# First gathers on edge numbers loaded for them alone, and a memset that follows only the first 190 early gathers, in a graph layer kernel

## The reference

```python
h = relu(layernorm(x))                                        # 100000 x 64
msgs_f = mlp_f([h[src], h[dst], edge_attr]); agg = segment_sum(msgs_f, dst)
msgs_r = mlp_r([h[dst], h[src], edge_attr]); agg += segment_sum(msgs_r, src)
return x + h + mlp_n([agg, h])                                # 100000 x 64
```

## Time and profile before

| what | value |
|---|---|
| runs | 1595.52, 1595.94, 1598.82 us; median 1595.94 |
| the profiled execution's own time | 1595.95 us |
| its span | 1594.2 us |
| POOL busy | 1102.0 us, 69% of the span |
| PE busy | 1280.9 us, 80% |
| DVE, ACT busy | 970.8 us, 942.6 us |
| DMA | 281.00 MB, 176 GB/s over the span |

### The profile page before, as it was taken

One profiled execution on the slowest core, in us unless ns is written; L12 is line 12 of the kernel. 1 busy time (PEld: TensorE's weight loads), 2 busy tenths in 40 slices (PEclk: granted clock), 3 DMA queues, 4 the chain that ended last, 5 costly groups with the idle time before them and its releaser, 6 DMA issues.

```text
span 1594.2 us, 29478 instructions
## 1 busy us (share of the span) xinstructions
PE 1280.9 (80%) x7070; PEld 969.6 (61%) x7070; DVE 970.8 (61%) x3294; ACT 942.6 (59%) x2256; POOL 1102.0 (69%) x1003
## 2 busy tenths in 40 slices
PE   5998998557888787878777788778678873999998
PEld 4777776335666565666555566556566652777776
DVE  7999999526666666666666666666666650222222
ACT  4888888434555455555455555555555442777776
POOL 7888888888888888888888888888888863000000
PEclk9999999767777888787888877877977786999999
DMA  6899998535555555555555555555555545999998
GB/s 217 292 315 315 314 315 279 161 49 111 111 112 111 111 99 102 104 104 103 105 105 105 105 104 99 106 102 99 101 102 105 104 78 156 382 370 369 364 367 297
DMA packets 238410, 281.00 MB, mean 176 GB/s; under 512 B 53170, under 2 KB 155200, under 8 KB 238348
## 3 DMA queue, kind: packets, MB, share of 16 engines
q1 hardware_dynamic: 168408, 241.57, 45.3%
q0 software_dynamic: 68992, 38.59, 21.5%
q10 hardware_dynamic: 948, 0.30, 0.1%
HBM read 162.62 MB, written 117.72 MB: 176 GB/s over the span
## 4 chain that ended last, share of the span: by engine, by line
POOL 36%; issue 21%; PE 18%; DMA 2%; DVE 1%; POOLq 1%; ACT 0%; ACTq 0%; DVEq 0%; SPq 0%
POOL table L532 30%; PE bank L871 6%; PE bank L882 6%; POOL got_odd L514 6%; PE bank L892 3%; DMA table<-to_send,scatter_at 2%; PE bank L820 1%; PE bank L846 1%; PE bank L818 1%; DVE same L979 0%; PE bank L833 0%; DMA same<-table 0%; ACT nh L639 0%; ACT to_send L625 0%; POOLq L530 0%
## 5 line engine op out<-in xcount | busy, mean ns | idle before, releaser
L532 POOL DMA_INDIRECT table<-to_send,scatter_at x392 | 623.5, 1591 | 134.7 <-issue 117.8
L846 PEld LDWEIGHTS bank<-message,same 128*128 128x128 f32 x1960 | 279.1, 229 | 45.6 <-issue 40.4
L846 PE MATMUL bank<-message,same 128*128 128x128 f32 x1960 | 300.2, 320 | 5.0 <-DVE message L1011 5.0
L639 ACT ACTIVATE nh<-nx,all_sums,all_rstd 128x64 f32<-128x64 f32 x784 | 280.3, 434 | 0.0
L514 POOL DMA_INDIRECT got_even<-in_x,gather_first x196 | 211.8, 1080 | 40.2 <-issue 35.0
L775 PE MATMUL bank<-wn_h,nturned 128*128 128x256 f32 x784 | 197.0, 395 | 31.7 <-ACT nhidden L683 24.1
L514 POOL DMA_INDIRECT got_odd<-in_x,gather_at x180 | 180.3, 1002 | 54.9 <-issue 54.9
L804 PE MATMUL bank<-ident,h_ends 128*128 128x128 f32 x196 | 51.4, 355 | 200.5 <-DVE h_ends L1020 185.6
L979 DVE TENSOR_SCALAR_CACHE_REDUCE same<-others,ids 128x128 f32<-128x128 int32 (+3 forms) x392 | 190.8, 543 | 12.7 <-DVE ids L971 7.5
L818 PE MATMUL bank<-turned,w_ends 128*128 128x256 f32 x392 | 167.8, 518 | 34.8 <-ACT turned_edge L609 34.8
L775 PEld LDWEIGHTS bank<-wn_h,nturned 128*128 128x128 f32 x784 | 143.5, 193 | 67.7 <-issue 37.9
(11 more groups left out here) (80 smaller groups left out, 1999.2 us busy)
## 6 DMA issues: line engine op xcount, KB each, us to landing
nx<-in_x SPq DMA_DIRECT2D x194, 256.0 KB
table<-nhidden SPq DMA_DIRECT2D x97, 512.0 KB
same<-table SPq DMA_DIRECT2D x97, 512.0 KB, 5.3
others<-numbers SPq DMA_DIRECT2D x196, 128.0 KB
out_x<-nh SPq DMA_DIRECT2D x79, 256.0 KB, 4.4
nx<-out_x SPq DMA_DIRECT2D x55, 256.0 KB, 4.4
out_x<-ncentred SPq DMA_DIRECT2D x49, 256.0 KB, 4.2
table<-to_send,scatter_at POOLq DMA_INDIRECT x392
```

What stands on the lines that cost most here:

```text
L532: pool.indirect_dma_start(table, bass.IndirectOffsetOnAxis(ap=scatter_at[s][:, k:k + 1], axis=0), to_send[s][:, k, :], None, compute_op=AL ...
L639: last = act.activation(nh[s][:, g, :], nx[place][:, g, :], ACT.Relu, bias=all_sums[:, at, g:g + 1].rearrange("p a g -> p (a g)"), scale=a ...
L846: last = pe.matmul(bank[6 + s][:, k * M:(k + 1) * M], same[s][:, o, k * P:(k + 1) * P], message[s][:, o, :], start=(o == k), stop=(o == KB ...
```

## The change

The first four gathers (batch 0) read a new tile `gather_begin`, 128 partitions by 2 by 2. It is filled by four DMAs of 128 numbers of 4 bytes, one number to a partition: two on SP's queue between the load of window 0 and `load_ends`, two on ACT's queue ahead of `load_ends`. They wait for nothing. POOL waits for these four before its first gather, and for `s_first` only before its fifth. The memset stands behind the first 190 early gathers, and ACT's `copy_sums` of the first batch waits for these 190. The other 18 early gathers follow one another directly.

```diff
+    PAUSED = 190
+        gather_begin = sb("gather_begin", [P, JT, 2], I32)
+        s_begin = sem("gather_begin_in")
+        def begin_ends(eng, end, a):
+            for j in range(JT):
+                eng.dma_start(gather_begin[:, j, end:end + 1],
+                              a[j * P:(j + 1) * P].rearrange("(p a) -> p a", a=1)).then_inc(s_begin, 16)
+
@@ sync, set_up
                 Step(NW, 0).do(load_x_begin, 0, ring=NRING)
+                begin_ends(sp, SRC, src)
                 load_ends(sp, SRC, src)
@@ gpsimd
-            pool.wait_ge(s_first, 1)
+            pool.wait_ge(s_begin, 2 * JT * 16)
             pauses = 0
             for b in range(NB):
                 i, s = divmod(b, 2)
-                at = gather_first[:, b * KB:(b + 1) * KB]
+                if b == 0:
+                    at = gather_begin[:, :, :].rearrange("p j e -> p (j e)")
+                else:
+                    at = gather_first[:, b * KB:(b + 1) * KB]
+                    if b == 1:
+                        pool.wait_ge(s_first, 1)
                 for k in range(KB):
                     if s == 0:
                         gather(got_even[:, i, :], at, s_got_even[i >= EARLY], [k])
@@
                     else:
                         continue
+                    if pauses == PAUSED:
+                        continue
                     if pauses:
                         pool.wait_ge(s_paused, pauses)
                     pool.memset(idle, 0.0).then_inc(s_paused, 1)
                     pauses += 1
@@ scalar
+            begin_ends(act, DST, dst)
             load_ends(act, DST, dst)
@@ scalar, copy_sums
                 elif s == 0:
-                    act.wait_ge(s_paused, KB * (PAIRS + LOOK))
+                    act.wait_ge(s_paused, PAUSED)
```

## The result

| what | before | after |
|---|---|---|
| runs (4 each) | 1595.45 to 1598.82, median 1595.73 us | 1583.49 to 1587.37, median 1586.33 us |
| ratio of after to before | | 0.9938, 95% interval 0.9925 to 0.9950 |
| the profiled execution, its span | 1595.95, 1594.2 us | 1586.92, 1585.2 us |
| POOL busy | 1102.0 us | 1094.1 us |

The changed kernel is 0.62% faster, 9.9 us by the ratio (8.0 to 12.0); 7.2 were forecast.

The account below looks back on a forecast made before the run. POOL's unbroken chain was taken to set the first scatter, and POOL's pace the edge loop. Savings of 3.0 us (earlier first gather) and 4.2 (18 gathers without memset) sum to 7.2: 1595.95 to 1588.7 us, range 1586.3 to 1592.3.

Parts of the forecast that it names:

- part 1: Start of POOL's chain: four small loads let the first gather start 3.3 us earlier, worth 3.0 us at the scatter.
- part 2: Last 18 early gathers without memsets: 1.29 us a period instead of 1.449 and a shorter gap before the scatter, saving 4.2.
- What bounds: POOL's unbroken chain to the first scatter, then the edge loop at POOL's pace: an earlier first scatter means an earlier end.
- I book no gain: Handover to the edge loop: ACT, DVE and PE work released earlier by ACT's shorter wait was counted as 0 us.
- theory R: From the experiments, not the prediction: the edge loop got 2.3 us shorter because ACT was released 20 us before the first scatter.
- Rival E: Edge loop: another phase against DVE copies could change each batch by 0.02, 2 us together either way; no chance of its own.
- A: Last early gathers: no quicker without the memset, the period stays 1.449; 4.6 us gained in all, 1591.4; chance 0.11.
- D: Last early gathers: a queue effect makes the period 1.6, costing 2.6 us; time 1594.0; chance 0.05.
- B: Start: the earlier first gather gains only 0 to 1 us, time 1591.7 to 1590.7; chance 0.10.
- Rival C: Last early gathers: the memset keeps POOL's descriptor queue from filling; unpaused gathers at 1.93 us cost 8.2, time 1599.6; chance 0.06.
- the 0 to 0.6 that was kept: Handover: allowance in the range for released DVE copies drawing out gathers, 0.19 us per copy.
- the row has it the other way: Gather at 302.55: against the skill's port-lock rule, the prediction read 0.19 us lost by the gather and none by DVE's copy.

Follow-up runs that it names:

- e6: Changed kernel with the four small loads kept, but the first gather held until the whole edge-number tile is ready, and 208 memsets; 1594.10 us, ratio 0.9998.
- e1: Kernel before with only the first edit: four gathers on numbers loaded for them alone, all 208 memsets kept; 1593.06 us, ratio 0.9965.
- e3: Changed kernel with one more memset behind the last early gather, which ACT waits for, so ACT is released late; 1587.92 us, ratio 0.9932.
- e2: Kernel before with only the second edit: 190 memsets and ACT's wait on 190; 1589.91 us, ratio 0.9950.
- e4: Kernel before with the memset on its own tile and ACT's wait for the memsets removed, all 208 memsets kept; 1596.76 us, ratio 0.9987.
- after_again: Changed kernel run a second time, unedited, on one chip with the others; 1583.67 us, ratio 0.9940.
- e5: Changed kernel with no memset at all and no wait of ACT for it; 1558.14 us, ratio 0.9773.
- f1: Changed kernel with no memset and no wait for it, repeated unedited on another occasion; 1558.40 us, ratio 0.9774.
- f2: Kernel before with no memset and no wait for it, second run of that program, one execution; 1558.14 us.
- f4: Changed kernel with each memset cut from 256 columns to 8, behind the same 190 gathers; 1558.86 us, ratio 0.9777.
- e10: Changed kernel with the memset behind only the first 120 early gathers; 1653.23 us, ratio 1.040.
- e8: Changed kernel with the memset behind only the first 75 early gathers; 1726.86 us, ratio 1.085.
- e7: Kernel before with no memset and no wait for it, and no separate loads for the first gathers; 1807.43 us, ratio 1.134.
- g1: Kernel before with no memset and no wait for it, third run of that program, on a further chip; 1557.51 us, ratio 0.9774.

## What the prediction had right, and which steps failed

Three terms of the sum of 7.2 were too small: the conversion of part 1 (3.0 booked, 4.2 measured in four profiles against four), the period of part 2 (4.2 booked, 4.6 to 4.7 measured), and the released work and the loop, booked at nothing (2.28 in the profiled pair, of which 0.8 in the first four batches). In that one pair part 1 gave only 2.61, so the pair's 9.03 owes a part to the loop's chance length. The ratio of 0.994 came again on another chip.

**What bounds.** Right. Every us that the first scatter came earlier is found at the end, up to the loop's own variation, and from the last scatter on it stayed at 259 to 260.4 us. The variation is large: e6's first scatter is at 341.11, 2.3 later than before's, and its median is within 0.2 of before's.

**Part 1, the first gather.** The bounds and the value held: 4.60 to 4.83 in the ten runs that start it early, 7.59 to 8.43 in the nine without the edit. The step that failed is the conversion, "3.3 / 1.602 = 2.06 more gathers, and these are missing later at 1.449". The extra gathers are not made at the slow pace: until 17.13 no gather of the kernel before was drawn out beyond the first, so they are made at 1.45 ahead of the begin stage's crowding. The 191st gather starts at 308.82, 306.33, 307.40 and 307.46 in the changed kernel's two profiles, e1 and e3, mean 307.5; at 311.43, 311.33, 311.01 and 312.96 in those without the edit (the kernel before twice, e2, e4), mean 311.7. That is 4.2 us, with about 1 us between single runs on either side, against the 3.0 of the forecast. The shift truly grows on the way. It is 3.2 at the first gather and 4.7 at the 41st: from the first to the 41st it takes 61.0 to 61.5 us in the four with the edit and 62.1 to 63.8 in the four without, and 8 of the gathers 2 to 40 are drawn out to 1.05 or more with it, 10 to 14 without. From there to the 191st the means give 0.5 back. The first profile of the changed kernel needs 242.99 us for that stretch, where its three likes need 240.5 to 241.5, which is why that pair shows 2.61. e6 goes the same way, with a first gather 1.5 late and a 191st 2.0 late.

**Part 2, the 18 gathers.** The mechanism was right in each piece: the gap of 0.30, ACT's copy out of the chain, its wait down from 35.6 to 5.7. The sum was 4.2, measured 4.66 here and 4.6 to 4.7 in after_again and e2. The mis-sized term is the period, 1.29 taken from the second gather of a pair; in a row it is 1.256 (0.95 and 0.30, rounded). The low bound of 1.26 was the better choice.

**"I book no gain"** for the released work, and theory R. The first four batches of the loop take 41.30 to 41.46 us where ACT is released late (both profiles of before, e1, e3) and 40.62 to 40.86 where early (both of after, e4, e5, f1, f2, f4). The 0.6 is mostly one scatter. In the late ones a scatter of the third batch takes 2.04 to 2.08 instead of 1.57, beside DVE's row addition `nh<-nx,nh`, and in after, after_again and e4 none of the first sixteen does. But e6, released late, has no such scatter and takes 40.93, and e2, early, has it and takes 41.12. So that the release did it is argued and not shown.

The rest of the loop's 2.28 belongs to no edit that the runs show. From the fifth batch to the 76th the changed kernel gains 1.7 at some 0.02 each, and from there it loses 0.2. Single batches of 10.6 to 10.7 instead of 10.15 come anywhere: e4 has eight of them, before five, after four.

With the terms as measured, 4.2, 4.6 and 0.6, the forecast would have been 9.4, and 1586.5 us.

**Rival E**, the loop, was given 2 us either way and no case; that was its size. **Rivals A and D** fell with the period of 1.26, and **B** with the first gather at 4.82 and the 191st 4.2 earlier. **Rival C**, that the memset keeps something from clogging, fell for these 18 gathers but was nearer to the purpose of the pauses than the forecast: with 88, 133 or 208 unpaused gathers beside the begin stage (e10, e8, e7) one chip gave 59, 133 and 213 us more. Its picture was wrong. The gathers don't get slower, they keep 1.256, and it is the begin stage that is held. The 18 did no harm on the chips where they ran, and the likely reason is another than C's odds: they stand behind the begin stage, whose last rows ACT copies at 288.

**What draws a gather out.** The prediction took the DVE copy within the gather at 302.55 for the cause of its 0.19. That reading was wrong, and the rows left the cause out. In the timeline of before, 0.11 ahead of that gather, stands

```profile
302.44 0.43 DVE L1020 SCALAR_TENSOR_TENSOR h_ends<-centred,rstd 128x256 f32<-128x256 f32 x1
```

The one drawn-out gather among the last 18, +0.17 and inside the 0 to 0.6 that was kept, has no copy in it. A row addition had started ahead of it instead. It is the same with the two long scatters of a batch of 10.7 in e4:

```profile
314.72 0.68 DVE L1066 TENSOR_TENSOR nsquares<-nx,nh 128x512 f32<-128x512 f32 x1
315.11 1.12 POOL L523 DMA_INDIRECT got_even<-in_x,gather_first  x1 [0.30 <-issue]
```

```profile
533.97 0.42 DVE L1018 SCALAR_TENSOR_TENSOR h_ends<-centred,rstd 128x256 f32<-128x256 f32 x1
534.02 1.83 POOL L532 DMA_INDIRECT table<-to_send,scatter_at  x1 [0.30 <-issue]
534.31 0.16 DVE L941 COPY gather_at<-gather_first 128x4 int32 x1
535.84 0.69 DVE L1047 TENSOR_TENSOR nh<-nx,nh 128x512 f32<-128x512 f32 x1
536.15 1.82 POOL L532 DMA_INDIRECT table<-to_send,scatter_at  x1 [0.30 <-issue]
```

In each a DVE instruction that reads two SBUF tiles is running when POOL's starts. Of the gathers from 10 to 302 us, 63 take 1.05 or more in the profile of before and 63 in that of after, and every one of them starts so. It is longer than 0.96 by what is left of the DVE instruction, less 0.12 to 0.13. No gather there that starts without one takes more than 0.97, also beside DVE's reductions, which read one tile. The eight scatters of the loop from 1.75 up in before, and the seven in after, start so too. The copies leave no mark of their own: of the 43 in e4 that fall into a scatter, 36 fall into one of 1.57 or 1.58, and the other seven stand behind an `h_ends` that had started ahead. The Trainium skill (SBUF — State Buffer, section "Who interferes with whom") has DVE and GpSimd share one port pair as an exclusive lock, which goes to whichever starts first; it names a DVE instruction with two SBUF inputs against a GpSimd instruction that reads SBUF. The traces agree with it, with these numbers, and the prediction's "the row has it the other way" falls with its reading. The rule doesn't explain the hold, which is in ACT's waits for PE: the same page gives both ports of their own.

**What stays open.** Why ACT stands for some 30 us at waits whose signals PE has long given, while gathers run unpaused; why on one chip of those tried and not on the others; and how long a pause prevents it. Also why the first edit leaves fewer of the first 40 gathers drawn out, beyond that their places against DVE's instructions are others. No version is given as better than both: e5, f1, f2, g1 and f4 are 2.3% faster where they aren't held, and e7 is 13% slower where it is. The changed kernel itself never ran on the chip of e7 to e10, so that its own 17 unpaused gaps are safe there is argued from their place, and not shown.

## What to carry to other kernels

If one engine's chain runs without a hole up to the start of the next stage, a shift of its start is worth its whole size (here 4.2 us at the end for 3.2 at the start), provided that the items gained are made before the crowding begins; convert it only at the pace of the place where they are made. To say what draws an instruction out, look at what the other engine had started ahead of it, and not only at what starts within it. A filler between instructions of an engine may guard another engine, as on one chip here: take it away first where the other stage is over, as here, and run the bolder version on several chips before trusting it. For an effect of a few us, count how far two profiles of the same kernel differ (here 2.7 us in one stage) before giving the rest to a cause.

## What the runs showed of the hardware that was not expected

- The same program took 1557 to 1558 us on two chips and 1807 us on a third, where the kernel before took 1594 on all three; the difference is whole stretches in which ACT stands for some 30 us at waits for PE, though PE's work for them had ended before ACT began to wait.
- In e7 the holds come at last every 33.6 us (DVE's reciprocal at 184.69, 218.31, 251.96, 285.49), and the last one outlives the gathers by 22.3 us, with no DMA packet moving from 289 to 300.
- A gather that starts while DVE is in an instruction with two SBUF inputs is drawn out by what is left of that, less 0.12 to 0.13 us (63 of 63 long gathers in each profile); where DVE starts 0.04 us or less ahead, the four cases in these two profiles have the gather at its plain 0.96.
- Gathers issued in a row take 1.256 us each (0.95 and 0.30, rounded); a memset of 8 columns between them adds nothing to that (0.96 + 0.12 + 0.18), one of 256 columns 0.19.
- Beside the begin stage, from the 81st to the 141st gather, the gathers fall into step with DVE's windows of 2.7 us: 1.61 a period with the long memset (after), five to three windows, and 1.34 without (e5), two to one.
